# Keys and queries of two 16-head cross-attentions turned by DMA instead of by TensorE, with scores nine slots ahead

## What is computed

```python
x = x + jnp.tanh(g_xattn[0]) * _L0_xattn_ref(_layernorm(x), ctx_768, mask_BxS_bk0, Wq, Wkv)
...
x = x + jnp.tanh(g_xattn[2]) * _L2_xattn_ref(_layernorm(x), ctx_768, Wq, bq, Wkv, bkv, Wo, bo)
...
q = (jnp.einsum('bld,ed->ble', x, Wq) + bq).reshape(b, l, h, dh)
k, v = (kv[..., :dh], kv[..., dh:])
att = jax.nn.softmax(jnp.einsum('blhd,bmhd->blmh', q, k) * scale, axis=2)
out = jnp.einsum('blmh,bmhd->blhd', att, v).reshape(b, l, d)
return jnp.einsum('bld,ed->ble', out, Wo) + bo
```

## Time and profile before

| | us |
|---|---|
| median of 3 runs | 1308.13 |
| lowest and highest run | 1302.78, 1309.09 |
| profiled execution, its span (first to last instruction) | 1291.0 |
| runs' median less this span (what lies around it) | 17.1 |
| x0, first to last instruction, about | 0 to 158 |
| x2, first product to the last of Wo, about | 743 to 910 |
| busy in the span: PE, DVE, POOL, ACT | 1097, 737, 654, 590 |

### The profile page before, as it was taken

One profiled execution on the slowest core, in us unless ns is written; L12 is line 12 of the kernel. 1 busy time (PEld: TensorE's weight loads), 2 busy tenths in 40 slices (PEclk: granted clock), 3 DMA queues, 4 the chain that ended last, 5 costly groups with the idle time before them and its releaser, 6 DMA issues. The chain is left out here.

```text
span 1291.0 us, 24027 instructions
## 1 busy us (share of the span) xinstructions
PE 1097.1 (85%) x8603; PEld 722.1 (56%) x8618; DVE 736.7 (57%) x2377; ACT 590.5 (46%) x1245; POOL 654.3 (51%) x1228
## 2 busy tenths in 40 slices
PE   8999645789999997999987968998998989993793
PEld 3444223347777873455445824553777757773693
DVE  5788387456545426887633357884455544445243
ACT  1687645245555443677421216877222345531220
POOL 5353183686655348654042644543223378647363
PEclk7799956899999995999757957998898989975897
DMA  4000090000000002000004499000100000001673
GB/s 137 19 2 2 14 130 2 0 2 1 1 1 1 1 1 73 1 2 3 1 25 150 138 158 143 5 2 2 47 1 1 1 1 1 2 19 45 189 221 134
DMA packets 54874, 54.19 MB, mean 42 GB/s; under 512 B 9787, under 2 KB 45905, under 8 KB 54758
## 3 DMA queue, kind: packets, MB, share of 16 engines
q1 hardware_dynamic: 49702, 44.75, 17.3%
q0 software_dynamic: 3712, 6.35, 1.5%
q10 hardware_dynamic: 1344, 1.57, 0.3%
HBM read 31.99 MB, written 21.97 MB: 42 GB/s over the span
## 5 line engine op out<-in xcount | busy, mean ns | idle before, releaser
L548 DVE TENSOR_REDUCE x_minus_max<-banks 128x2 f32<-128x512 f32 x256 | 167.8, 686 | 39.4 <-PE banks L534 37.4
L556 ACT ACTIVATE x_probs<-banks 128x512 f32<-128x512 f32 x256 | 145.5, 597 | 52.0 <-PE banks L540 49.8
L534 PE MATMUL banks<-x_kT,x_qT 32*128 32x256 bf16 x512 | 95.2, 303 | 15.9 <-DVE x_minus_max L548 9.5
L1843 DVE CUSTOM_DVE_ANT_0 x_work<-banks,hide_later_keys 128x128 f32<-128x128 f32 (+1 forms) x256 | 79.8, 352 | 27.0 <-PE banks L1956 25.5
L540 PE MATMUL banks<-x_qT,x_kT 32*128 32x256 bf16 x512 | 87.2, 284 | 3.6 <-ACT x_probs L556 3.4
L1887 ACT ACTIVATE x_work<-banks 128x384 f32<-128x384 f32 x128 | 62.6, 495 | 57.9 <-PE banks L1962 57.3
L1260 DVE TENSOR_REDUCE x_minus_max<-banks 128x2 f32<-128x512 f32 x64 | 43.2, 686 | 56.8 <-PE banks L1517 56.8
L573 PE MATMUL banks<-x_probs,x_v_with_ones 128*32 128x256 f32 x1024 | 71.1, 397 | 2.9 <-ACT x_probs L556 2.9
L534 PEld LDWEIGHTS banks<-x_kT,x_qT 32*128 32x128 bf16 x512 | 27.4, 95 | 77.3 <-DVE x_minus_max L548 43.1
L1547 PEld LDWEIGHTS banks<-x_v_with_one,x_probs 128*128 128x128 f32 x512 | 60.4, 192 | 5.6 <-issue 5.6
L3566 POOL DMA_INDIRECT f_returned_rows<-f_tile_out,f_tile_rows x46 | 45.3, 984 | 34.4 <-issue 19.0
(11 more groups left out here) (616 smaller groups left out, 3032.6 us busy)
## 6 DMA issues: line engine op xcount, KB each, us to landing
f_sorted_rows<-f_row_without_home SPq DMA_DIRECT2D x10, 845.0 KB, 21.1
w_f_moe<-in_f_experts SPq DMA_DIRECT2D x11, 578.0 KB, 4.0
f_sorted_rows<-f_row_without_home SPq DMA_DIRECT2D x5, 903.0 KB, 22.5
y_resident<-in_f_w SPq DMA_DIRECT2D x10, 384.0 KB
f_tile_rows<-f_sorted_rows SPq DMA_DIRECT2D x23, 130.0 KB, 2.7
w_f_wg<-in_f_w SPq DMA_DIRECT2D x5, 384.0 KB, 3.5
w_f_wu<-in_f_w SPq DMA_DIRECT2D x4, 384.0 KB
w_f_wd<-in_f_w SPq DMA_DIRECT2D x4, 384.0 KB, 3.9
```

What stands on the lines that cost most here:

```text
L534: mm = nc.tensor.matmul(K.PS[:, SMAX0 + m % 2, t * S:(t + 1) * S], h["qT"][r, c % 3, g, t * P:(t + 1) * P], h["kT"][r, c % 3, g, :], start ...
L548: K.nc.vector.tensor_reduce(h["nm"][:, b % 2, :, n], K.PS[:, SMAX0 + n % 2, :].rearrange("p (t n) -> p t n", t=T), AX_X, ALU.max, negate=T ...
L556: K.nc.scalar.activation(h["p"][:, n % (2 * HG)], K.PS[:, ST0 + n % 2, :], ACT.Exp).then_inc(s["p"].sem, 1)
L1843: ins = nc.vector.tensor_tensor_reduce(unused[:, m % 2, t, 0:w], K.PS[:, TOP + m % 2, t * P:t * P + w], hide[:, t, 0:w], -1.0, -HIDE, ALU. ...
```

## The change

- **The turn.** PE's 24 transposes of a batch, ACT's copy L481 and DVE's copies L486 and L491 go. Instead SP issues three DMA transposes in a batch, SBUF to SBUF, 128 x 1024 bf16 each (`sp_turn`). The order on SP is: keys of batch c, queries of batch c, then queries with maxima of batch c-1. Keys of c wait for all probabilities of batch c-3 (its buffer is the same), then for `ke`; the queries wait for `qe`. `kT` and `qT` change their layout to match, and the score products read them in the same sizes.
- **Lag.** CROSS_LAG = 9 in place of LAG = 6. The first score of batch c stands in slot 7 of batch c-2, before in slot 10.
- **Places.** Projections and splits move up. PE: rows turned in slot 7, keys and values in 8, queries in 11, all of the batch three ahead. POOL: normalised rows in slot 3, maxima placed in 7, splits in 14 and 15. In x2 the turn of the output goes to slot 9 and the product with Wo to 13.
- **Unread products.** The two of each batch of x0 are gone; those before the steady part (HELD0) stay.
- **Other queues.** In x0 SP issues six weight loads after the turns of each batch instead of all at the start. The ten clearing DMAs of f3 move from beside x2 to the block of x1, behind f0.
- Some semaphores are shared between stages; bank MISC is named FIRST and MISC + 1 is named KV.

```diff
-    return (b + 1, n + LAG) if n + LAG < H else (b + 2, n + LAG - H)
+    return (b + 1, n + lag) if n + lag < H else (b + 2, n + lag - H)
...
+def sp_turn(K, sp, h, rows, turned, b, landed):
+
+    K.nc.sync.dma_start_transpose(h[turned][:, b % 3].rearrange("p t g n -> p (t g) n"),
+                                  h[rows][:, b % 2].rearrange("p h e -> p (h e)")).then_inc(landed.sem, 16)
...
         if m == 0:
-            pe.wait_ge(s["kT"].sem, s["kT"].after(c))
-            pe.wait_ge(s["qT"].sem, s["qT"].after(c))
+            pe.wait_ge(s["kT_in"].sem, s["kT_in"].after(c))
+            pe.wait_ge(s["qT_in"].sem, s["qT_in"].after(c))
...
         if n == 0:
-            pe.wait_ge(s["qmT"].sem, s["qmT"].after(b))
+            pe.wait_ge(s["qmT_in"].sem, s["qmT_in"].after(b))
...
-            if n == 13 and alive(b + 1):
-                pe_turn_q_and_max(K, pe, s, h, b + 1)
...
-            if wo is None and alive(b):
-                last = min(c, B - 1)
-                if n in (9, 12):
-                    pe.wait_ge(s["kT"].sem, s["kT"].after(last))
-                    pe_keep_busy(K, h, b, MISC)
...
+    def sync(sp, between=nothing):
+
+        for b in range(-2, B):
+            c = b + 2
+            if alive(c):
+                if c >= 3:
+                    sp.wait_ge(s["p"].sem, s["p"].after(c - 3))
+                sp.wait_ge(s["ke"].sem, s["ke"].after(c))
+                sp_turn(K, sp, h, "ke", "kT", c, s["kT_in"])
+                sp.wait_ge(s["qe"].sem, s["qe"].after(c))
+                sp_turn(K, sp, h, "qe", "qT", c, s["qT_in"])
+            if alive(b + 1):
+                sp.wait_ge(s["qm"].sem, s["qm"].after(b + 1))
+                sp_turn(K, sp, h, "qe", "qT", b + 1, s["qmT_in"])
+            between(sp, b)
...
             @block.sync
             def _(sp):
                 m1_later(sp)
-                clear_rows(sp, K.f3_region, K.no_row[:], CLEARED3, "region_cleared")
+                x2_turns(sp)
```

More of the change, by code:

```diff
@@ L343 @@
 LAG = 6
+CROSS_LAG = 9
 MIX_SLOT = 6
@@ L435, in pool_split_k @@
 def pool_split_k(K, pool, s, h, b):
+    if b >= 2:
+        pool.wait_ge(s["kT_in"].sem, s["kT_in"].after(b - 2))
     pool_split(K, pool, s, h, b, "ks", "ke", slice(0, 3, 2), 1)
@@ L767, in tensor @@
         for b, n in slots(3):
-            c = b + 2
-            if load_all is not None and (b, n) == (-2, 1):
+            if load_all is not None and (b, n) == (-3, 11):
                 pe_hold_clock_early(K, OUT0, HEAD_HOLDS[1])
@@ L777, in tensor @@
                 pe_mix_group(K, pe, s, h, *group)
-            if n == 0 and alive(c):
+            c = b + 3
+            if n == 7 and wo is not None and alive(b - 2):
+                pe.wait_ge(s["rows_out"].sem, s["rows_out"].after(b - 2))
+            if n == 7 and alive(c):
+                pe.wait_ge(s["xn"].sem, s["xn"].after(c))
+                for t in range(T):
+                    mm = nc.tensor.transpose(K.PS[:, FIRST, t * P:(t + 1) * P], K.norm["xn"][:, c % 2, t], K.ident[:])
+                mm.then_inc(s["xnT_ps"].sem, 1)
@@ L844, in _ @@
                 def _(sp):
-                    load_all(sp)
+                    rest = load_all(sp)
+                    next(rest)
+                    turns(sp, lambda sp, b: advance(rest, LOADS_EACH))
+                    finish(rest)
             @block.gpsimd
@@ L3719, in build, with fetch_each @@
         groups = {}
+        def fetch_each(sp, group, *more):
+            for name in WEIGHTS:
+                if name[:2] == group and name not in EXPERT:
+                    fetch(sp, group, W[name][:], a[name])
+                    yield
+            for dst, src in more:
+                fetch(sp, group, dst, src)
+                yield
         def fetch(sp, group, dst, src):
```

184 lines of the change are left out of this document (81 added, 103 removed).

## The result

The changed kernel takes 1350.74 us (median of 6 runs, 1336.60 to 1389.24); the kernel before, run beside it, 1307.89 us (6 runs, 1297.72 to 1314.88). The ratio is 1.0239, 95% interval 1.0175 to 1.0303: slower, with a median outside the forecast's range of 1292 to 1342. Ratios in this document compare fast executions alone, and that of the changed kernel rests on its three quickest (1336.6 to 1342.3 us), while the median takes in all six and the profile is of one of the three slow ones (1359.2). Among the runs of the changed kernel the time follows the clock: 1336.6 us at a mean granted clock of 0.846, 1359.2 at 0.821, 1389.1 at 0.794. The profiled execution has a span of 1357.4 us for 1291.0 before, so its 66.4 us are twice what the ratio says, some 31 us of 1308.

The account below looks back on a forecast made before the run. No engine alone; score, maximum and exponential through two banks set a 3.18 us quad floor. Batches save 8.2 (x0) and 5.5 (x2), starts cost 5.7 each: 2.3 off, 1305.8 us; range 1292 to 1342.

Parts of the forecast that it names:

- For the clock PE's own work must do: x2 never had such products: Steady batches: PE's remaining work keeps the clock up without unread products; no time counted for losing it.
- The six weight loads ... land before the next turns are issued, some 10 us later: x0's loads behind the first turns, 8.4 us to land in such a queue, would not delay the next turns.
- The start of each stage, +5.7: Starts of x0 and x2: about +2.8 to the first score and +2.9 to the first ST product, each stage.
- T = 3.5, L = 4.7: Steady batches: one DMA turn takes 3.5 us, two in a row 4.7; no stall for a pair up to 5.4.
- Rivals 2 and 3: Steady batches: the pair of turns becomes the period, 1336 us, chance 0.23; or blocks are served one by one, 1420, 0.05.
- The quads of x0, 13.13: Steady x0: a batch's four quads sum to 13.13 us against 14.3; 8.2 us off the stage.
- The quads of x2, 14.06: Steady x2: a batch's four quads sum to 14.06 us against 14.72; 5.5 us off the stage.
- The clearing DMAs, 0: Moving them from beside x2 to beside x1: nothing counted either way, 1 us each way kept for the range.
- rival 4: Steady batches: the change does nothing there and only the starts cost, 1319 us, chance 0.10.
- rival 1: x0 and x2: fewer PE waits or the clock back sooner, 3 to 6 us more gained each, say 1297; chance 0.22.

Follow-up runs that it names:

- e5: Changed kernel with x2 put back as in the kernel before, so only x0 turns by DMA, without unread products: 1326.2 us, ratio 1.0183.
- e7: Changed kernel plus the 24 old PE transposes per steady batch of x2, their results unread: 1338.8 us, ratio 1.0201.
- e12: Changed kernel plus two unread 512-column products in each steady batch of x2 alone: 1339.6 us, ratio 1.0240.
- e15: Changed kernel with x0's weight loads issued after its last turn, no unread products in its batches: 1341.9 us, ratio 1.0282.
- e13: Changed kernel with x0's loads behind its last turn, unread products ahead of both stages' first scores and two per batch: 1323.3 us, ratio 1.0157.
- e14: e13 with scores six slots ahead instead of nine and maxima placed after slot 10: 1329.6 us, ratio 1.0215.
- e17: Changed x0 with unread products ahead and two per batch, three weights loaded mid-stage, other loads last; x2 as in kernel before: 1315.3 us, ratio 1.0031.
- e9: Kernel before without x0's two unread products per batch, and with the clearing DMAs moved beside x1: 1305.5 us, ratio 1.0049.
- e16: e14 without the two unread products per batch, those ahead of the first scores kept: 1322.7 us, ratio 1.0149.
- e2: Changed kernel with SP issuing weight loads only from the first steady batch of x0 on: 1341.3 us, ratio 1.0263.
- e18: Changed x2 with unread products ahead of first scores and two per batch; x0 turned on PE without unread products: 1313.4 us, ratio 1.0035.
- e4: Changed kernel with both the four unread products of e1 and the later weight loads of e2: 1330.1 us, ratio 1.0208.
- e1: Changed kernel plus four unread 512-column products in each steady batch of both stages: 1328.1 us, ratio 1.0155.
- e11: e4 with scores six slots ahead instead of nine and maxima placed after slot 10: 1329.3 us, ratio 1.0145.

## Why the prediction was wrong, by its own steps

- **"For the clock PE's own work must do: x2 never had such products".** This step failed. That x2 had no unread products before showed only that its 24 transposes a batch were enough beside the rest. The change took these away, and I asked what they cost, not what they kept up. In the steady batches the clock never fell with the transposes on PE (12 stages) or with unread work in their place (17), and it fell in 6 of 11 without, for up to 91.9 us. In the profiled execution that is 47.6 of 66.4 us. By the ratios x2 is the smaller part, since x0 alone costs 1.8 of 2.4% (e5). The same step failed in x0: its batches took 118.9 us or more in the traces of e5, e7, e12 and e15, for 116.0 before, and 110.2 to 113.9 where the start and the batches had unread products and the turns a clear queue (e13, e14, e17). The spans of x2 alone would not have shown it: those with unread work run from 119.5 to 137.5 us, those of the old x2 from 121.7 to 130.2, those without work 130.6, 134.5, 170.9 and 179.9.
- **"The six weight loads ... land before the next turns are issued, some 10 us later".** Failed. The next turn was issued 7.7 us behind the first load and 3.2 behind the last one, and held its queue for 10.31 us. I had the load's 8.4 us and put the wrong distance beside it.
- **The start of each stage, +5.7.** In x2, counted from the first turned rows, it was 2.2 to the first maximum (9.8 for 7.6) and 3.6 to the first exponential, 5.8 us: right. In x0 it was mis-sized, 14.4 (15.6 in e5): the first score stood at 19.55 and the first ST product at 51.82, where 18 and 43 were said. Without loads among the turns the first exponential came 4.1 us sooner (e15, 48.4 for 52.5), and with unread products ahead of the scores as well another 6.0 (e13, 42.4), with half clock for 14.6 us of it in place of 28.6. What is left over the old 38.1 is 4.3, near what I had counted.
- **T = 3.5, L = 4.7.** Right, a little high: 3.0 to landing, and 1.24 more for the second of a pair. No steady batch of the changed kernel waited. Rivals 2 and 3 fell with it. What the Trainium skill says on the page "Advanced Engine Details and Errata", section "X-Bar Transpose (TRN2)", that such transposes are as fast as ordinary DMAs, is borne out for this shape: the plain 256 KB rows took 2.3 and 3.5 us. Eight times the 1309 ns that the Trainium skill gives on the page "VectorE: DVE Perf Modes", section "The three transpose paths", would be 10.5 us, and is not.
- **The quads of x0, 13.13.** Mis-sized by 0.4: 3.62, 3.49, 3.22 and 3.18. At full clock four pairs and a mix group take 2.28 us of PE, not 2.13 (a bare slot is 0.32, the group 1.00), and the query projection 0.65, not 0.55. The old batch was mis-read too, 14.3 for the 14.56 that every steady batch of that trace took, so the two errors nearly cancel: 1.05 us saved a batch for 1.17. The step's mechanism was right where the clock held: x0's exponentials took 7.8 us less (8.2 said) in the profiled execution, which was luck, since they took 2.9 and 6 us more with the same code in e5, e7 and e12.
- **The quads of x2, 14.06.** Mis-sized, and so the gain is not there. Five groups, four quads, of x2 at full clock in e15:

```profile
837.39 1.07 PE L575 MATMUL banks<-x_probs,x_v_with_ones 128*32 128x256 f32 x16
841.48 1.07 PE L575 MATMUL banks<-x_probs,x_v_with_ones 128*32 128x256 f32 x16
845.64 1.07 PE L575 MATMUL banks<-x_probs,x_v_with_ones 128*32 128x256 f32 x16
848.74 1.07 PE L575 MATMUL banks<-x_probs,x_v_with_ones 128*32 128x256 f32 x16
851.92 1.07 PE L575 MATMUL banks<-x_probs,x_v_with_ones 128*32 128x256 f32 x16
```

  The four quads are 4.09, 4.16, 3.10 and 3.18, 14.5 for 14.7: the work that left PE was in other quads than the work that came, and with projection, half and Wo together (2.28 + 0.65 + 0.58 + 0.65 = 4.16) one quad is PE's alone.
- **The clearing DMAs, 0.** Right (e9).
- **The rivals.** Rivals 2 and 3 named a wait for DMA as the cause, and rival 4 said that only the starts cost. None had the clock as a cause, though rival 1 let it come back sooner. A slower case with a stage at half clock in its batches belonged among them.

Open is why the unfilled x2 held its clock through the steady batches in e15 and e16 and not in the changed kernel and e2; how long it was at half clock in the executions that weren't profiled; and some 0.9% between e13 (1.0157) and what e17 and e18 cost together, since f0 starts late in e17 too. e17 makes four edits in x0 at once, and how its 1.5% divides among them is read from traces of one execution each.

## What to carry to other kernels

Work that leaves TensorE is also work that kept its clock: before taking it away, compare the granted clock of the stages that have it with the stretches that don't, and price the case in which the lower level stays (here 14.7 to 23.9 us a batch). A DMA that an engine waits for does not belong on a queue in which large loads are issued ahead of it; moving the loads by a batch moved the wait by a batch here, and leaving them for the end kept SP in the block for 5 us after the others were done. Where the time of a kernel varies with the clock, profile more than one execution before saying which stage holds a loss. Do the sum of PE's work by quads, or whatever the natural ruler is, for where the work lands and not only for how much leaves.

## What the runs showed that I had not expected

PE can be busy without a gap and still be kept at half clock. In e4, for instance, 15 us at a stretch in the first batches of x0:

```profile
50.00:65.00 15.00, 15.00 (x92) 5.60 (x91) 7.71 (x15) 8.00 (x16) 5.48 (x13) 0.50 0.32 92
```

Unread products are not free there: the third quad of x0's first batch, at half clock, took 4.98 us in e1 and 4.39 in e5, which has none. A DMA transpose of 128 x 1024 bf16 from SBUF to SBUF holds SP for 1.24 us and lands in 3.0, but behind loads it held its queue for 10.3 us and landed after 15.3 (18.4 in e11).
